# Weight sums moved to GpSimd, weight forms split one pair earlier, and tiles 1 and 2 of the down stage prepared ahead of the last gatings

## The reference

```python
def lora_add(base, inp, A, B):
    Ab = A[layer_idx][lora_indices]
    Bb = B[layer_idx][lora_indices]
    t = jnp.einsum('bri,bni->bnr', Ab, inp)
    return base + jnp.einsum('bor,bnr->bno', Bb, t) * SCALE
gate = lora_add(jnp.einsum('bnh,fh->bnf', x, W_gate), x, A_gate, B_gate)
up = lora_add(jnp.einsum('bnh,fh->bnf', x, W_up), x, A_up, B_up)
act = jax.nn.silu(gate) * up
down = lora_add(jnp.einsum('bnf,hf->bnh', act, W_down), act, A_down, B_down)
...
x = x + down
x = x + jnp.einsum('bct,bcd->bdt', x, weights[condition])
```

## Time and profile before

| | us |
|---|---|
| median of 3 runs | 457.99 (457.64 to 458.76) |
| the profiled execution | 457.48 |
| its span | 455.6 |
| PE busy | 437.4 (96% of the span) |
| DVE busy | 335.0 (74%) |
| ACT busy | 213.3 (47%) |
| GpSimd busy | 168.2 (37%) |

### The profile page before, as it was taken

How to read it: one execution, slowest core, us unless ns; L and a number is a source line. 1 busy time by engine, 2 the same in 40 slices (tenths; PEclk the granted TensorE clock), 3 DMA queues, 4 the chain that set the end, 5 groups by cost and what they waited for, 6 DMA issues and landing times.

```text
span 455.6 us, 7248 instructions
## 1 busy us (share of the span) xinstructions
PE 437.4 (96%) x2465; PEld 393.9 (86%) x2465; DVE 335.0 (74%) x621; ACT 213.3 (47%) x396; POOL 168.2 (37%) x156
## 2 busy tenths in 40 slices
PE   5999999977999999999999999988999999999997
PEld 4978988865898888888888888988999999999996
DVE  6778698876876866967867857976766676676665
ACT  6664334365436335444444444925434545433441
POOL 3612120120311211111111551675566676665630
PEclk9999999999899999999999999999999999999999
DMA  8965663325667467466475589787556666555631
GB/s 268 378 221 150 182 181 108 104 81 147 167 170 210 109 163 193 112 199 157 112 205 148 141 260 337 196 201 201 170 173 192 205 199 202 176 175 175 201 104 46
DMA packets 99699, 81.12 MB, mean 178 GB/s; under 512 B 50928, under 2 KB 83056, under 8 KB 99664
## 3 DMA queue, kind: packets, MB, share of 16 engines
q1 hardware_dynamic: 88368, 47.27, 37.1%
q0 software_dynamic: 11008, 33.30, 24.0%
q10 hardware_dynamic: 288, 0.10, 0.1%
HBM read 65.18 MB, written 15.47 MB: 177 GB/s over the span
## 4 chain that ended last, share of the span: by engine, by line
PE 86%; DVE 7%; DMA 2%; ACT 2%; issue 1%; SPq 1%; DVEq 0%; ACTq 0%
PE bank L1300 24%; PE bank L1146 9%; PE bank L1147 9%; PE bank L1148 8%; PE bank L1191 8%; PE bank L1192 8%; PE bank L1193 8%; PE bank L1214 4%; PE bank L1213 4%; PE bank L1330 2%; DVE wd L763 2%; DMA actT_raw<-actT_dram 2%; PE bank L1310 1%; DVE b_gu L767 1%; PE bank L1315 1%
## 5 line engine op out<-in xcount | busy, mean ns | idle before, releaser
L441 POOL DMA_INDIRECT b_raw<-in_b_rows,rows x48 | 50.8, 1059 | 199.3 <-DVE b_gu L767 198.7
L1300 PE MATMUL bank<-wd,actT_hi 128*128 128x288 f32 x648 | 112.0, 295 | 3.1 <-DVE actT_lo L763 1.9
L1300 PEld LDWEIGHTS bank<-wd,actT_hi 128*128 128x128 f32 x648 | 95.5, 188 | 4.7 <-issue 3.5
L441 POOL DMA_INDIRECT a_dn_raw<-in_a_dn_rows,rows x64 | 75.5, 1180 | 19.5 <-issue 19.5
L767 DVE SCALAR_TENSOR_TENSOR b_gu<-b_raw,low_rows,b_gu 128x1024 fp32r<-128x1024 f32 (+1 forms) x48 | 55.6, 1159 | 30.6 <-ACT b_gu L500 30.6
L1300 PE MATMUL bank<-wd,actT_lo 128*128 128x288 f32 (+1 forms) x324 | 69.4, 296 | 0.0
L1300 PEld LDWEIGHTS bank<-wd,actT_lo 128*128 128x128 f32 (+1 forms) x324 | 51.9, 188 | 0.0
L500 ACT ACTIVATE b_gu<-b_raw 128x1024 fp32r<-128x1024 f32 (+1 forms) x48 | 46.2, 963 | 12.2 <-DMA b_raw<-in_b_rows,rows 10.7
L585 ACT ACTIVATE act<-bank 128x512 f32<-128x512 f32 (+1 forms) x48 | 26.2, 547 | 44.1 <-PE bank L1214 43.9
L763 DVE TENSOR_TENSOR actT_lo<-actT_raw,actT_hi 128x1280 fp32r<-128x1280 f32 (+1 forms) x32 | 27.0, 885 | 15.5 <-ACT actT_hi L500 14.6
L872 DVE TENSOR_TENSOR act<-act,bank 128x512 f32<-128x512 f32 (+1 forms) x48 | 29.9, 622 | 8.1 <-PE bank L1214 7.3
(11 more groups left out here) (177 smaller groups left out, 993.8 us busy)
## 6 DMA issues: line engine op xcount, KB each, us to landing
actT_raw<-actT_dram SPq DMA_DIRECT2D x16, 640.0 KB
actT_dram<-staging SPq DMA_DIRECT2D x64, 128.0 KB, 2.8
x_sb<-in_x SPq DMA_DIRECT2D x16, 256.0 KB, 2.9
xT_raw<-in_xT SPq DMA_DIRECT2D x15, 256.0 KB, 3.0
out<-out_sb SPq DMA_DIRECT2D x15, 256.0 KB, 2.0
a_raw<-in_a_gu_rows SPq DMA_DIRECT2D x56, 64.0 KB, 2.4
actT_dram<-staging SPq DMA_DIRECT2D x32, 88.0 KB, 3.1
wd_raw<-in_w_down SPq DMA_DIRECT2D x10, 256.0 KB, 7.1
```

The lines of the kernel that those rows point to most:

```text
L441: return pool.indirect_dma_start(dst, None, src, bass.IndirectOffsetOnAxis(ap=rows[:, tile, col:col + 1], axis=0))
L1300: last = pe.matmul(ps_down[e][half][:, 0:HALF], a[e][0:n, c, :], wd[0:n, c, part, at:at + HALF], start=(c == 0 and i == 0), stop=(c == NC ...
```

## The change

The eight weight sums go from DVE to GpSimd, in pair 1, between the gathers there (`pair_with_sums`). The forms are split in the order t2, t1, t4, t3, the first six pieces in pair 1 (before: two), t3 in pair 2 ahead of `split_s`. On PE, in the first product after a wait for `b_ready`, the wait goes behind the weight products. At the end, five chunks of W_down are split in pair 7 (before: four), between its additions; the gatings of units 4 and 5 go behind tile 1's splits (DVE: behind `mask_td(0)`); PE starts tile 1 after the gating of unit 3 (before: unit 5), takes three chunks of hi products ahead of lo ones there too (`first_chunks`), and mixes in tile 1 at chunk 9 (before: 7); SP loads tile 2 ahead of one load of x and of the last spill.

```diff
-SPLITS = [(f, m) for f in ("t2", "t3", "t1", "t4") for m in MATRICES]
+SPLITS = [(f, m) for f in ("t2", "t1", "t4", "t3") for m in MATRICES]
...
@@ SyncE, behind pair 7 @@
             load_x(0, 0)
+            load_actT(2, 0)
             load_x(1, 1)
             spill(PAIRS - 1, 2)
-            load_actT(2, 0)
...
@@ GpSimd @@
+            def sum_weights(f, i):
+                if f == "t3":
+                    pool.wait_ge(w_ready, GU_PIECES)
+                elif f != "t1":
+                    pool.wait_ge(weights_summed, 4 if f == "t2" else 6)
...
+                nc.gpsimd.tensor_tensor(block_raw(f, m), block_raw(a, m), block_raw(b, m), ALU.subtract)\
+                    .then_inc(weights_summed, 1)
...
@@ ScalarE, split_forms @@
                         sc.wait_ge(weights_summed, 6)
-                    elif f == "t1":
-                        sc.wait_ge(w_ready, GU_PIECES + i)
-                        sc.wait_ge(weights_summed, 8)
                     elif f == "t3":
                         sc.wait_ge(xT_used[1], PLAIN)
-                    else:
+                    elif m == "up":
+                        sc.wait_ge(w_ready, GU_PIECES + i - (1 if f == "t1" else 0))
+                        sc.wait_ge(weights_summed, 8)
+                    elif f == "t4":
                         sc.wait_ge(w_ready, GU_PIECES + i)
...
@@ TensorE, fast_pair @@
-                pe.wait_ge(b_ready[0], NS * pr + 2)
                 for i, m in enumerate(MATRICES):
                     pe.wait_ge(p1_copied, fast(pr, i))
                     p2 = product(ps[m][0][:, :], xT_hi[0], xT_lo[0], 1, "b21", m, False)
                     if i:
                         p2.then_inc(xT_used[0], 1)
+                    else:
+                        pe.wait_ge(b_ready[0], NS * pr + 2)
                     lora_half(ps[m][0][:, :], 0, i, PIECE)
...
-            down(0, 0, first=True)
-            pe.wait_ge(act_ready, NU * PAIRS)
-            down(1, 1)
+            down(0, 0, early=True)
+            pe.wait_ge(act_ready, NU * (PAIRS - 1) + 4)
+            down(1, 1, early=True)
```

More of the change, by code:

```diff
@@ L482, in _ @@
             gather_b(0, 0, 1)
-            for pr in range(PAIRS):
+            pair(0)
+            pair_with_sums(1)
+            for pr in range(PLAIN, PAIRS):
                 pair(pr)
@@ L929, in fast_pair @@
                 split_b(pr, 0, 1)
-                if first:
-                    split_forms(2, 4)
                 split_b(pr, 1, 0)
                 if first:
+                    split_forms(6, 8)
                     split_s(pr)
                 gating(pr, 1)
-                if first:
-                    split_forms(4, 6)
-                else:
-                    split_b(pr, 1, 1)
+                split_b(pr, 1, 1)
                 gate(pr, 2)
+                if last:
+                    split_down(0, 1)
                 add_u3(pr, 0)
-                if not first:
-                    turn(pr, 2)
+                turn(pr, 2)
                 add_u3(pr, 1)
-                if first:
-                    turn(pr, 2)
-                    split_forms(6, 8)
-                    split_b(pr, 1, 1)
                 if not last:
                     split_x(pr + 1, 0)
+                else:
+                    split_down(1, 2)
                 add_u7(pr, 0)
+                if last:
+                    split_down(2, 3)
                 add_u7(pr, 1)
@@ L1078, in residual_out, with down @@
                 nc.vector.tensor_tensor(out_sb[e][:, :], x_sb[e][:, :], ps_mix[:, 0:H], ALU.add).then_inc(out_ready, 1)
-            def down(m, e, first=False, last=False):
-                if not first:
-                    mask_td(m - 1, 1 - e)
-                    split_mix(m - 1, 1 - e)
+            def down(m, e, last=False):
+                mask_td(m - 1, 1 - e)
+                split_mix(m - 1, 1 - e)
                 if not last:
                     split_a_dn(m + 1, 1 - e)
-                if not first:
-                    residual_h(m - 1, 1 - e)
+                residual_h(m - 1, 1 - e)
                 if not last:
@@ L1093, in down @@
                 split_b_dn(m, e)
-                if not first:
-                    residual_out(m - 1, 1 - e)
+                residual_out(m - 1, 1 - e)
             split_a_dn(0, 0)
             split_actT(0, 0)
-            split_down(4, NC)
+            split_down(5, NC)
+            split_a_dn(1, 1)
+            split_actT(1, 1)
+            split_b_dn(0, 0)
+            mask_td(0, 0)
             gating(PAIRS - 1, 4)
-            split_a_dn(1, 1)
             gating(PAIRS - 1, 5)
-            split_actT(1, 1)
-            ve.wait_ge(s_used, FAST)
-            split_b_dn(0, 0)
-            down(1, 1)
+            split_mix(0, 0)
+            residual_h(0, 0)
+            split_a_dn(2, 0)
+            split_actT(2, 0)
+            split_b_dn(1, 1)
+            residual_out(0, 0)
             down(2, 0)
@@ L1268, in fast_pair @@
                         p3.then_inc(s_used, 1)
+                    else:
+                        pe.wait_ge(b_ready[0], NS * pr + 3)
                     lora_half(ps[m][3][:, :], 0, i, PIECE)
```

102 lines of the change are left out of this document (54 added, 48 removed).

## The result

The changed kernel takes **466.16 us** (median of four runs, 465.57 to 466.44) where the kernel before takes 458.13 beside it: ratio 1.0173, 95% interval 1.0155 to 1.019. That is 8.0 us slower; the forecast was 2.8 slower. The profiled span is 463.8 us against 455.6.

A forecast was written before the change was run, and what follows sets the result against it. PE is busy in 437.4 of 455.6 us, so the time is PE's work plus its waits. Start of pair 2 +10.0, middle -4.0, end -3.2, together +2.8: forecast 460.8 us, range 455.2 to 468.5.

The forecast's parts named there:

- The chain of forms: Start of pair 2: three dependent form splits ahead of gate(1,4) make PE wait at base(2,1), 3.6 us lost.
- The 0.8 more for the tT of tile 0: Start of pair 2: PE reaches the lora at 93.6, tile 0's tT comes at 94.4, 0.8 us lost.
- The middle: Middle of pair 2: waits of 2.31 and 3.43 and slow clock 1.7 become waits 0.9 and 2.5, gain 4.0 us.
- The sums on GpSimd: Pair 1: at 3.2 us a sum and 1.3 in front, the sixth sum ends at 78.4, 3.9 us lost.
- my own bound: Pair 1: the sixth sum may end at 74.5; each microsecond beyond it is lost at PE.
- rival 2: Pair 1: DVE's two-operand SBUF pieces and GpSimd's sums wait for each other, 7.7 us more, 468.5; chance 0.24.
- The prices from a page: GpSimd sums by the skill's figures: 2.3 us a sum, 6 in front, sixth ends at 77.7, 3.2 us lost.
- The clock: Start of pair 2: PE waits of some 7 us are followed by the slow clock, 1.7 us added.
- The end: Tiles 1 and 2 of down: the waits of 1.91 and 1.20 go, with 0.1 of restart, gain 3.2 us.
- The price of a chunk between the additions: Pair 7: W_down chunks between the additions cost nothing, up to 0.7 us if ACT's part comes late.
- Rival 1: Sums come in time, pair 2 loses only the chain of forms: 455.2, or 456.9 with slow clock; chance 0.25.
- rival 3: Pair 1: GpSimd's sums at their upper bound, 5.5 us more, 466.3; chance 0.08 with worse.

The follow-up runs named there:

- experiment 1: The changed kernel with the eight weight sums back on DVE at their old places in pair 1; 461.39 us, ratio 1.0073 to the kernel before.
- experiment 5: The kernel before with only the end of the change, 456.77 us; the same with the mix of tiles 0 and 1 at chunk 7, 456.06 us.
- experiment 2: The kernel before with only the eight weight sums moved to GpSimd in pair 1; 468.94 us, ratio 1.0213.
- e13: The kernel before with end kept, b_gu waits and split moved, t4 up's piece behind xT_lo, pair 3's a_raw loads issued early in pair 2; 449.24 us.

## Why the prediction was right and wrong

The direction held, and the time lies inside the range; the size did not, 8.0 for 2.8. Point by point, by its own steps:

- **The chain of forms** (3.6 ahead of base(2,1)): right. Where nothing else disturbs it, the wait is 3.85 (experiment 1), 3.61 with copies or memsets. The 0.8 more for the tT of tile 0 did not come in any profile. The forecast added it to the 1.7 of the clock, but the second leaves no room for the first: behind each of these waits the clock was slow, PE took 4.0 to 4.9 us to that lora in place of 2.63, and the tT (3.3 us behind base(2,1)'s start in the changed kernel) was there first.
- **The middle**: the two waits are as worked out, 0.94 for 0.9 and 2.35 for 2.5. What failed is the condition put behind it, "if a wait of 2.5 us leaves the clock alone as that of 2.31 did". In the profiled execution it did not hold: the window 118 to 120 has 0.54, so about 1.5 of the 4.0 was not won. In the six profiles with this wait (2.33 to 2.38) the slow clock followed in three and stayed away in three, so a single number for it is luck either way. Nor had I asked what is late next once the middle is shorter: 1.32 and 1.16 at the start of pair 3 in experiment 1. In the changed kernel itself these do not show.
- **The sums on GpSimd** (3.9 lost by their pace): the step that failed. The price of a sum was too high (3.2, measured 2.37) and so was the 1.3 in front (0.1). By my own bound the sixth sum might end at 74.5; it ended at 74.54, after GpSimd had stood for 2.8 us at the gather of 68.81, for a b_gu that came late behind tT_lo. So their pace cost nothing. Yet they cost 4.8 us by the medians, because they hold DVE. The place of that was given as rival 2, with two misreadings: that each of DVE's instructions waits for *the sum under way* and then takes its turn (they wait for the whole run), and that the harm lies at t2's pieces and b_gu. It began at tT_lo, an instruction of 0.42 us that I had not looked at because it is short: 2.96 us of PE in pair 1. The two b_gu, which rival 2 does name, brought the other part, 2.5 of the 6.36 ahead of base(2,1) (against 3.85 in experiment 1); t2's pieces were not held at all, since they start behind the last sum. From the Trainium skill, SBUF — State Buffer, § Who interferes with whom, too, I had taken "the whole instruction" for the unit; the traces show 9.36 us, four instructions.
- **The prices from a page.** The figure of the Trainium skill, GPSIMD Engine Reference, § Performance versus the Vector engine, scales to an estimate of 2.25 us for a sum, close to the 2.37 measured. By its § Instruction dispatch some 6 us would lie ahead of the first one; the first sum starts 0.1 us behind the gather, so no such cost shows here.
- **The clock** (1.7 for one slow stretch in place of another): the profile has two against one, +1.9. The timed executions say the same: the mean granted clock of the changed kernel was 0.985, 0.989, 0.989 and 0.992, that of the kernel before 0.996 in 23 of 49.
- **The end** (3.2): the waits of tiles 1 and 2 went in the changed kernel, but 0.49 for h_lo came, and by itself the end gives 1.4 to 1.9. The price of a chunk between the additions, which I let run from nothing to 0.7, is 0.63 in experiment 5 and nothing in the changed kernel.

In the sum of waits the forecast was not far off (+2.9 worked out, +4.25 found), but that is luck: 3.9 for a pace that cost nothing and 0.8 for a wait that never came stand where 5.5 of the hold belong; the clock (0 for 1.9) and what no edit moves (the first 34 us) make up much of the rest of the 8.0. Rival 1 fell: the sums were in time, and it still did not become 455.2, since "in time" was the wrong test. The time is that of rival 3 (466.3) by accident; the reason is a wider form of rival 2's.

## To carry over

Before you move elementwise work to GpSimd, list every DVE instruction beside it that reads two SBUF operands, the short ones too: each may stand until the whole run of GpSimd's reading instructions is over. Ask of each microsecond won on the critical path which load, issued at its old time, is late next. And where a stall comes from one semaphore, move the wait behind the work that doesn't need it before reordering whole engines: two such edits, with the loads moved and the end of the change kept, gave 9 to 10 us (449.00 against 458.15 over all executions of the kernel before, ratio 0.9775 beside it) where the change lost 8.

## What was not expected of the hardware

- The hold of DVE by GpSimd lasts over back-to-back reading instructions (four sums 9.36, two 6.09 and 4.74, four copies 3.84) and across a memset of 0.09 us between them; it ends when GpSimd is idle (2.38). GpSimd's memset holds nothing (0.43), and DVE's turn, which reads one tile, is not held by a sum (0.71).
- The same wait is not always followed by the slow clock. In the profiles here, from pair 1 to the end of pair 3, every PE wait of 3.4 us or more was followed by a stretch at 1.2 GHz (11 of 11), of those between 1.9 and 3.1 us 7 of 14, and none below 1.6; of the three waits of 1.9 to 2.1 us that open tile 1 of down one was (experiment 2). That of 2.31 us, with the same code ahead of it, shows both:

```profile
100.00:102.00 2.00, 2.00 (x7) 1.54 (x6) 1.90 (x5) 0.42 (x1) 1.00 (x1) 0.60 0.28 16
102.00:104.00 2.00, 2.00 (x7) 1.58 (x6) 0.98 (x1) 0.98 (x2) 0.00 (x0) 0.55 0.76 241
```

  This is the kernel of experiment 5 behind 99.45; in the kernel before the clock stayed at full speed there. It is what spreads the times of one kernel: 49 executions of the kernel before have a mean clock of 0.996 (23, mean 457.4 us), 0.992 or 0.993 (18, 459.0) or 0.988 or 0.989 (8, 460.2), some 1.5 us a step, while e13, with no wait over 0.94 us between the first 35 us and its last tile, stays within 0.7 us.
